# Attention with mixture of experts: row sums once a quarter, pair sums on VectorE, three jobs moved to ScalarE

## The reference

```
xn = layernorm(x)
q, k, v = xn @ W.T + b                      # 16 heads of 32
s = q.k / sqrt(32), causal, minus slope[h] * |i - j|
attn = (softmax(s) @ v) @ Wo.T + bo
logits = xn @ gate_w.T; top 2 of softmax(logits), their weights normalised
ffn = sum over both: weight * (silu(xn @ w1g.T) * (xn @ w1u.T)) @ w2.T
out = x + attn + ffn
```

## Time and profile before

| | |
|---|---|
| median of 3 runs | 1599.04 us (1596.22 to 1602.14) |
| profiled execution | 1600.13 us, span 1598.3 us |
| TensorE busy | 1465.1 us, 92% of the span |
| VectorE busy | 936.9 us, 59% |
| ScalarE busy | 703.9 us, 44% |
| GpSimd busy | 848.4 us, 53% |
| groups 0 to 14 | from 75 to 1068 us |
| last group, then its tail | 1068 to 1118 us, then to about 1175 us |

### The profile page before, as it was taken

How to read it: one execution, slowest core, us unless ns; L and a number is a source line. 1 busy time by engine, 2 the same in 40 slices (tenths; PEclk the granted TensorE clock), 3 DMA queues, 4 the chain that set the end, 5 groups by cost and what they waited for, 6 DMA issues and landing times.

```text
span 1598.3 us, 35194 instructions
## 1 busy us (share of the span) xinstructions
PE 1465.1 (92%) x13499; PEld 862.9 (54%) x13499; DVE 936.9 (59%) x1765; ACT 703.9 (44%) x1179; POOL 848.4 (53%) x732
## 2 busy tenths in 40 slices
PE   4689989998998999999999899897789999999995
PEld 2356555654655565555565456553356565655663
DVE  7667877766687666668768976560143333333331
ACT  5245565545556555556664444465022222222221
POOL 5134555444454454545564446575117777668774
PEclk9899998999998999999999999998899999999998
DMA  7244433443524426343233310233867888889983
GB/s 252 57 130 135 140 94 108 119 132 105 161 81 116 136 85 209 92 126 102 89 107 112 100 41 16 68 126 101 303 161 131 133 129 137 125 120 148 147 138 44
DMA packets 189309, 193.92 MB, mean 121 GB/s; under 512 B 104900, under 2 KB 138948, under 8 KB 189021
## 3 DMA queue, kind: packets, MB, share of 16 engines
q1 hardware_dynamic: 160636, 152.27, 35.6%
q0 software_dynamic: 26128, 37.24, 14.0%
q10 hardware_dynamic: 2384, 2.16, 0.4%
HBM read 93.14 MB, written 53.74 MB: 92 GB/s over the span
## 4 chain that ended last, share of the span: by engine, by line
PE 67%; DVE 11%; DMA 8%; ACT 4%; issue 4%; POOL 3%; SPq 2%; ACTq 0%; another core or an unknown queue 0%; DVEq 0%; POOLq 0%
PE S L1356 13%; PE T L1205 4%; PE S L1205 4%; PE M L1284 4%; PE O L1387 4%; PE M L1387 4%; PE S L1238 3%; DVE arena L1671 3%; PE T L1238 3%; PE S L1266 3%; DMA arena<-arena 3%; PE O L1284 3%; DMA out<-arena 2%; PE T L1222 2%; PE T L1318 2%
## 5 line engine op out<-in xcount | busy, mean ns | idle before, releaser
L1864 ACT ACTIVATE arena<-S,psl 128x512 f32<-128x512 f32 (+1 forms) x640 | 401.8, 642 | 359.2 <-PE S L1268 194.4
L1984 POOL TENSOR_TENSOR arena<-arena 128x1024 f32<-128x1024 f32 (+1 forms) x160 | 312.3, 1954 | 215.9 <-ACT arena L1864 215.4
L2038 POOL DMA_INDIRECT out<-arena x142 | 222.1, 1564 | 110.2 <-issue 46.7
L1356 PE MATMUL S<-arena 128*128 x1704 | 267.4, 314 | 6.1 <-issue 4.9
L1671 DVE TENSOR_REDUCE arena<-S 128x1 f32<-128x512 f32 (+3 forms) x311 | 202.8, 656 | 103.5 <-PE S L1243 53.2
L1671 DVE TENSOR_REDUCE arena<-T 128x1 f32<-128x512 f32 (+3 forms) x297 | 193.7, 656 | 87.1 <-PE T L1243 49.1
L1356 PEld LDWEIGHTS S<-arena 128*128 128x128 f16 x1704 | 166.8, 98 | 103.7 <-issue 7.4
L1266 PE MATMUL S<-arena 106*128 106x256 f16 x640 | 179.3, 280 | 22.4 <-ACT arena L1864 21.2
L1973 POOL TENSOR_TENSOR arena<-arena 128x512 f16<-128x512 f32 x64 | 78.9, 1233 | 153.9 <-DVE arena L1644 153.7
L1783 DVE COPY arena<-T 128x512 f16<-128x512 f16 x71 | 30.2, 425 | 219.8 <-PE T L1371 181.9
L1238 PE MATMUL T<-arena 105*128 105x512 f16 (+3 forms) x382 | 113.1, 333 | 25.0 <-DMA arena<-in_up 10.1
(11 more groups left out here) (218 smaller groups left out, 2517.3 us busy)
## 6 DMA issues: line engine op xcount, KB each, us to landing
arena<-arena SPq DMA_DIRECT2D x192, 128.0 KB, 2.8
arena<-in_w1T SPq DMA_DIRECT2D x64, 352.0 KB, 3.6
arena<-in_x SPq DMA_DIRECT2D x64, 256.0 KB, 4.4
w_d<-arena SPq DMA_DIRECT2D x32, 352.0 KB, 2.8
arena<-w_d SPq DMA_DIRECT2D x16, 704.0 KB, 6.7
arena<-in_w2T SPq DMA_DIRECT2D x32, 256.0 KB, 3.0
out<-arena SPq DMA_DIRECT2D x32, 256.0 KB, 3.2
xn_d<-arena SPq DMA_DIRECT2D x24, 256.0 KB, 2.6
```

The costliest lines, as they stand in the source:

```text
L1356: tp = pe.matmul(y[:, i * 512:i * 512 + I], xT[:, s % XDEEP, 4 * a + c, :], weights[:, bass.ds(reg[s] + (w_ * NX * W1N + c * 2 * I + i * I ...
L1864: act.activation(PT[t % 3][:, h, 0:n], CB[o.bank["score", u]][:, 0:n], ACT.Exp, scale=psl[:, hh:hh + 1]).then_inc(sems["exp"], 1)
L1984: pool.tensor_tensor(PS[t % 3][:, :, f:f + n], PT[t % 3][:, :, f:f + n], PT[t % 3][:, :, c:c + n], ALU.add).then_inc(sems["add"], 1)
L2038: pool.indirect_dma_start(out=halves, out_offset=bass.IndirectOffsetOnAxis(row[:, part, s:s + 1].bitcast(U32), 0), in_=yo[:, s % YDEEP, c0 ...
```

## The change

- `rsum` is made once a quarter instead of once a quad: of AC, the sum over all key blocks of the quarter. It is placed right behind the first product with V of the next quarter; for the very last quad it stays where it was.
- GpSimd still adds the key halves of each quad: for the first of a quarter straight into AC (two buffers), for the others into PSF (off the diagonal) or PSD (diagonal). On the diagonal it has two instructions of 128x512 where it had one.
- New step `acc` on VectorE for all quads but the first of a quarter, placed at u + 4: AC += PSF (128x1024), or the right half of AC += PSD (128x512).
- `vsb` and `qkh` move from VectorE to ScalarE. V is copied without its bias. New step `aTh` on ScalarE adds the bias (`bvs`) to the quotient, twice (128x256 each): rounded into aT and in place; GpSimd's `aT` keeps only the subtraction.
- `aTh` comes a unit behind `a32`, `aT` another; `inverse` comes 4 units behind `osb` instead of 3. `wsl` comes a unit later, its store doesn't.
- The broadcast of the V bias at the start and its buffer go; buffers shift by 512 words, which moves one expert weight load from window 3 to window 4.

```
@@ score, products, sums @@
             at(u + 1, lambda: add("add", t))
+            if i:
+                at(u + 4, lambda: add("acc", t))
             at(4 * t + 5, lambda: products(t))
-            at(4 * t + (10 if i < q else 9), lambda: sums(t))
+            if t == QUADS - 1:
+                at(4 * t + 9, lambda: sums(t))
...
         add("pv", t)
+        if i == 0 and t:
+            sums(t - 1)
...
         add("rsum", t)
-        if i == q:
-            at(now[0] + 1, lambda: emptied(G, q))
+        at(now[0] + 1, lambda: emptied(G, q))
@@ emptied @@
-                add("aT", G, q)
-                ready["aT", G, q] = now[0] + 2
+                at(now[0] + 1, lambda: add("aTh", G, q))
+                at(now[0] + 2, lambda: add("aT", G, q))
+                ready["aT", G, q] = now[0] + 4
...
-        at(now[0] + 3, inverse)
+        at(now[0] + 4, inverse)
@@ w_split @@
             yield
+            yield
             add("wsl", i)
-            for _ in range(2):
-                yield
+            yield
             add("wstore", i, sem="wd", inc=16)
@@ sync @@
-                    sp.dma_start(bvb[:, :], T["bv"].partition_broadcast(P)).then_inc(sems["bb"], 16)
@@ tensor, rsum @@
+                if i:
+                    on.wait_ge(*at("acc", t))
                 for x in range(4):
-                    R = YB[o.bank["pv", G, q]][D * x:D * x + D, 2 * P:4 * P]
-                    if i < q:
-                        tp = pe.matmul(R, ones, PS[t % 3][:, x, :], start=False, stop=False)
-                    else:
-                        pe.matmul(R[:, 0:P], ones, PT[t % 3][:, x, 0:P], start=False, stop=False)
-                        tp = pe.matmul(R[:, P:2 * P], ones, PS[t % 3][:, x, P:2 * P], start=False, stop=True)
+                    tp = pe.matmul(YB[o.bank["pv", G, q]][D * x:D * x + D, 2 * P:4 * P], ones, AC[q % 2][:, x, :],
+                                   start=False, stop=True)
@@ vector @@
+            elif kind == "acc":
+                t, = key
+                G, q, i = quad(t)
+                on.wait_ge(*at("add", t))
+                f, z = (0, PSF) if i < q else (P, PSD)
+                if i > 1:
+                    on.wait_ge(*at("acc", t - 1))
+                dve.tensor_tensor(AC[q % 2][:, :, f:], AC[q % 2][:, :, f:], z, ALU.add).then_inc(sems["acc"], 1)
@@ scalar @@
+                act.activation(st[:, 2 * qk, lo:hi], t32_at(*key), ACT.Copy).then_inc(sems["qkh"], 1)
...
+                act.activation(V[(G + 1) % 3][:, 4 * half:4 * half + 4, :].rearrange("p a n -> p (a n)"),
+                               PB[o.bank["v", b, g, half]][:, :], ACT.Copy, scale=col(CV)).then_inc(sems["vsb"], 1)
...
+                on.wait_ge(*at("a32", G, q))
...
+                a_ = osb[:, q % 2, 0:2 * P]
+                act.activation(aT[:, 0, g, 2 * q * P:2 * (q + 1) * P], a_, ACT.Identity, bias=bvs[:, g:g + 1])
+                act.activation(a_, a_, ACT.Identity, bias=bvs[:, g:g + 1]).then_inc(sems["aTh"], 1)
@@ gpsimd, add @@
+                if i == 0:
...
+                    f, n = (0, 2 * P) if q else (P, P)
+                    if q == 0:
+                        pool.tensor_copy(z[:, :, 0:P], y[:, :, 0:P])
+                    pool.tensor_tensor(z[:, :, f:f + n], y[:, :, f:f + n], y[:, :, 2 * P:2 * P + n],
+                                       ALU.add).then_inc(sems["add"], 1)
+                elif i < q:
+                    if t > 10:
+                        on.wait_ge(*at("acc", t - 1 if i == 2 else t - 3 if q == 3 else t - 6))
+                    elif i == 2 or q == 3:
+                        on.wait_ge(*at("acc", t - 1 if i == 2 else t - 3))
+                    pool.tensor_tensor(PSF, y[:, :, 0:2 * P], y[:, :, 2 * P:4 * P], ALU.add).then_inc(sems["add"], 1)
+                else:
+                    if G or q > 1:
+                        on.wait_ge(*at("acc", t - (3, 3, 4)[q - 1]))
+                    pool.tensor_tensor(PSD, y[:, :, P:2 * P], y[:, :, 2 * P:3 * P], ALU.add)
...
+                    pool.tensor_tensor(z[:, :, 0:P], z[:, :, 0:P], y[:, :, 0:P], ALU.add).then_inc(sems["add"], 1)
@@ gpsimd, aT @@
-                then(pool.tensor_copy(d0, osb[:, q % 2, 0:2 * P]))
                 pool.tensor_tensor(d1, osb[:, q % 2, 0:2 * P], d0, ALU.subtract).then_inc(sems["aT"], 1)
```

More of the change, by code:

```diff
@@ L878, in build @@
     xh, to = place(to, [P, 3, 2 * E], F16)
-    bvb, to = place(to, [P, E], F32)
     EARLY = to
@@ L886, in build @@
     PT1, to = place(to, [P, 4, 512], F32)
-    PS0, to = place(to, [P, 4, 2 * P], F32)
+    AC0, to = place(to, [P, 4, 2 * P], F32)
     RAWO_AT = to
-    PS1, to = place(to, [P, 4, 2 * P], F32)
+    AC1, to = place(to, [P, 4, 2 * P], F32)
     V2, to = place(to, [P, 8, P], F32)
@@ L893, in build @@
     AFTER_PT = to
-    PS2, to = place(to, [P, 4, 2 * P], F32)
+    PSF, to = place(to, [P, 4, 2 * P], F32)
+    PSD, to = place(to, [P, 4, P], F32)
     V1, to = place(to, [P, 8, P], F32)
@@ L1635, in vector @@
                                   PB[o.bank["gate", b]][:, 0:64], col(IG), None, ALU.mult).then_inc(sems["lg"], 1)
-            elif kind == "qkh":
-                b, g, qk, half = key
-                lo, hi = half * 512, half * 512 + 512
-                on.wait_ge(*at("qk32", *key))
-                if b * NG + g:
-                    gb, gg = (b, g - 1) if g else (b - 1, NG - 1)
-                    for h in range(4):
-                        on.wait_ge(*at("stack", gb, gg, h))
-                dve.tensor_copy(st[:, 2 * qk, lo:hi], t32_at(*key)).then_inc(sems["qkh"], 1)
-            elif kind == "vsb":
-                b, g, half = key
-                on.wait_ge(*at("v", b, g, half, 3))
-                on.wait_ge(sems["bb"], 32)
-                G = b * NG + g
-                if G > 2:
-                    on.wait_ge(*at("pv", 10 * (G - 2) - 1))
-                elif G == 2:
-                    on.wait_ge(*at("place", 1))
-                    on.wait_ge(*at("place", 2))
-                elif G == 1:
-                    on.wait_ge(*at("wol", 1))
-                dve.scalar_tensor_tensor(
-                    V[(G + 1) % 3][:, 4 * half:4 * half + 4, :],
-                    PB[o.bank["v", b, g, half]][:, :].rearrange("p (a n) -> p a n", a=4), col(CV),
-                    bvb[:, g * P:(g + 1) * P].unsqueeze(1).to_broadcast([P, 4, P]), ALU.mult,
-                    ALU.add).then_inc(sems["vsb"], 1)
             elif kind == "mx":
@@ L1843, in scalar @@
                                scale=cs).then_inc(sems["qk32"], 1)
+            elif kind == "qkh":
+                b, g, qk, half = key
+                lo, hi = half * 512, half * 512 + 512
+                on.wait_ge(*at("qk32", *key))
+                if b * NG + g:
+                    gb, gg = (b, g - 1) if g else (b - 1, NG - 1)
+                    for h in range(4):
+                        on.wait_ge(*at("stack", gb, gg, h))
+                act.activation(st[:, 2 * qk, lo:hi], t32_at(*key), ACT.Copy).then_inc(sems["qkh"], 1)
+            elif kind == "vsb":
+                b, g, half = key
+                on.wait_ge(*at("v", b, g, half, 3))
+                on.wait_ge(*at("scales", 1))
+                G = b * NG + g
+                if G > 2:
+                    on.wait_ge(*at("pv", 10 * (G - 2) - 1))
+                elif G == 2:
+                    on.wait_ge(*at("place", 1))
+                    on.wait_ge(*at("place", 2))
+                elif G == 1:
+                    on.wait_ge(*at("wol", 1))
+                act.activation(V[(G + 1) % 3][:, 4 * half:4 * half + 4, :].rearrange("p a n -> p (a n)"),
+                               PB[o.bank["v", b, g, half]][:, :], ACT.Copy, scale=col(CV)).then_inc(sems["vsb"], 1)
+            elif kind == "aTh":
+                G, q = key
+                b, g = G // NG, G % NG
+                on.wait_ge(*at("a32", G, q))
+                if b:
+                    on.wait_ge(*at("o", b - 1, 2 * q, 2))
+                    on.wait_ge(*at("o", b - 1, 2 * q + 1, 2))
+                a_ = osb[:, q % 2, 0:2 * P]
+                act.activation(aT[:, 0, g, 2 * q * P:2 * (q + 1) * P], a_, ACT.Identity, bias=bvs[:, g:g + 1])
+                act.activation(a_, a_, ACT.Identity, bias=bvs[:, g:g + 1]).then_inc(sems["aTh"], 1)
             elif kind == "exp":
@@ L1851, in scalar @@
                     on.wait_ge(*at("add", t - 3))
-                    if quad(t - 3)[1] == quad(t - 3)[2]:
-                        on.wait_ge(*at("rsum", t - 3))
                 elif t == 2:
```

28 lines of the change are left out of this document (14 added, 14 removed).

## The result

The changed kernel took 1609.07 us (median of 4 runs, 1606.28 to 1610.55), the kernel before beside it 1597.88 us (4 runs); the ratio is 1.0088, 95% interval 1.0054 to 1.0123. So it is slower by 0.9%, where the prediction had 1554 us, 2.8% faster. The profiled span is 1608.3 us against 1598.3.

A forecast was written before the change was run, and what follows sets the result against it. TensorE, busy 95% of the attention stage, was taken as the bound. 59.4 + 3 + 1 + 2 - 9 - 8 - 2 - 1 = 45.4 us off 1600.13 gave 1554.7, set at 1554 us; range 1536 to 1580.

The forecast's parts named there:

- 59.4 us: Attention, TensorE: fewer row-sum sets save 59.4 us over the 15 groups that TensorE bounds.
- the rival that TensorE's gain isn't the time's: Attention: exponential, GpSimd sum and maxima set the pace together, so gaps just grow; 1592 to 1600 us, chance 6%.
- -8 us: Attention, VectorE: net +51 us of work makes TensorE wait longer for the maxima, 8 us lost.
- The rival in which the lock makes VectorE the bound: Attention: every `acc` waits out a whole GpSimd sum on the shared SBUF port; 1625 us, chance 4%.
- hidden: Attention, GpSimd: net +49 us of work costs no time, since its sums wait for exponentials anyway.
- -9 us: Attention, ScalarE: 160 inserted instructions, one in ten delaying an exponential without slack, lose 9 us.
- the second rival: ScalarE's `aTh`, in the exponentials' queue, waits for the normalised rows instead of GpSimd; 1577 us, chance 20%.
- +3: Attention, TensorE: row-sum sets of off-diagonal quads stop waiting for GpSimd's sums, 3 us gained.
- +1: One queue entry less at the start and roundings off VectorE while it is saturated, 1 us gained.
- +2: Last group: the reciprocal placed later means less waiting for the fold ahead of the exponentials, 2 us gained.
- -2: Routing's split low part comes a unit later, its store doesn't, leaving less time to land: 2 us lost.
- All of it arrives: Attention: slack swallows VectorE's and ScalarE's added loads, and the last group gains too; 1533 us, chance 15%.

The follow-up runs named there:

- run 9: Kernel before with row-sum sets only for diagonal quads, 64 instead of 160, multiplying a constant; 1565.70 us, 0.982.
- run 10: run 9 plus, in `acc`'s place, a one-input VectorE sum along the row that waits for its GpSimd sum; 1601.21 us, 1.003.
- run 4: Changed kernel with the 48 large `acc` cut from 128x1024 to 128x4, order and semaphores kept; 1578.99 us, 0.9917.
- run 2: Kernel before with only the moves: `qkh`, `vsb` and the two additions of `aTh` on ScalarE; 1593.27 us, 0.9994.
- run 12: run 9 plus the three moves to ScalarE; 1562.64 us, 0.9792.
- run 1: Changed kernel without the moves: `qkh` and `vsb` back on VectorE, `aT` back on GpSimd alone; 1614.28 us, 1.0121.
- run 7: run 6 without the moves, the V copy as in run 1; 1641.82 us, 1.028.
- run 6: Changed kernel without `acc`: GpSimd adds both halves of every quad to the running sum, moves kept; 1627.16 us, 1.0207.
- run 11: run 9 plus GpSimd's extra sums, the diagonal pair sums of 48 later quads made twice; 1572.66 us, 0.9869.
- run 3: Changed kernel with `aTh` directly behind `a32` and `aT` one unit earlier; 1617.51 us, 1.0136.
- run 8: Changed kernel with the spreading product `bc` and what follows (`a32`, `aTh`, `aT`) two units earlier; 1619.33 us, 1.0144.
- run 5: Changed kernel with the 48 large `acc` as one-input sums along the row of the same 128x1024; 1604.15 us, 1.0061.
- run 14: Changed kernel with every `acc` one unit earlier in VectorE's queue; 1643.54 us, 1.0288.

## Why the prediction was wrong, point by point

**The row sums, "59.4 us".** This is the first step that failed. The count of the sets and their cost were right to a sixth (50.7 of 59.4 us): TensorE's busy time fell by 50.7 us in run 9. But the step took TensorE's time for the kernel's. Run 9 gives 30.6 us (1596.32 to 1565.70), with VectorE, ScalarE and GpSimd doing the work that they did before. The prediction read 53 us of gaps in 993 as "TensorE is the bound"; it set a chance of 6% on the rival that TensorE's gain isn't the time's. About half of that rival is what happens: the gaps grow by a third of the saving (16.9 of 50.7 us) even before any engine gets more to do. A small sum of waits tells how often the others are late now, not how soon they would be.

**VectorE, "-8 us".** This step failed by more, and it turned the sign. The durations were good: `acc` was put at 1.59 and 0.80 us and took 1.415 and 0.905, 111.4 us in all against 114.7. The price was not: run 10 sets it at 35.5 us for 63 us more busy time in the stage (70 in the span), and run 4 gives 27 us back for 54. That is some 0.5 us of time for 1 us of VectorE, waits included, at an engine busy 72 to 78% of the stage. Of the 40 us by which run 10's stage is longer, 15.7 are TensorE's own busy time at the lower mean clock, the rest its gaps. The prediction had -8 for a net load of 51 us, 0.16 for 1, by letting the 23.2 us of waits grow by a third; they grew to 55.1 us. It also set the rounding and V copies that leave VectorE against `acc` one for one. The runs say that they are worth much less: in runs 2 and 12 VectorE loses 69 to 71 us (and GpSimd some 23) and the time 0 to 3 us, with ScalarE's load of some 90 us as the other side. Where VectorE or GpSimd has more to do, the same moves give more: 5 us from run 1 to the change, not clear of noise, and 12 us from run 7 to run 6, which is. Whether a gain on VectorE and a loss on ScalarE cancel was not tried by itself; the waits point to it (TensorE's waits from run 9 to run 12, for VectorE 35.0 to 28.5 us, for ScalarE 25.4 to 40.2 us; from run 1 to the change, 72.9 to 55.1 and 22.0 to 42.7).

**The lock.** Its row was read rightly, but for one figure: L1725 was through 0.76 us after the sum (462.12 against 461.36), not 0.95. The rival in which the lock makes VectorE the bound did not come: `acc` would have had to average 3 us, and its mean is 1.16. Undisturbed (the medians, 1.21 and 0.68 us) the 96 would be 90.7 us, so by this estimate the lock adds 20.7 us to them. It strikes others as well, the 128x1 at 347.44 and the layer norm's L1553 at 239.97; both stand ahead of maxima. In sum that is nothing new for L1553: its 32 have a mean of 850 ns here and 924 in the kernel before. The Trainium skill says in SBUF — State Buffer, section "SBUF: two separate sides", that the one who comes second on the shared port pair stands still for the other's whole instruction; both rows agree: L1704 took 2.21 us for one element per partition beside a sum with 2.20 us to go, and L1553, which takes 0.54 us undisturbed (its median), was through 0.29 us after its sum.

**GpSimd, "hidden".** The load was 69 us in the whole span (49 predicted), and run 11 prices 58 us of it, in the stage, at 7.0 us. Runs 6 and 7 show the same with more. In the time this is a small miss, but the reason given, that GpSimd waits for exponentials anyway, doesn't hold where its instructions hold up VectorE.

**ScalarE, "-9 us", and the second rival.** The additions took 0.50 us, not 0.40, and ScalarE's busy time grew by 96 us in the span, not 113. TensorE waits 32.7 us for the exponentials, close to the 35 that the prediction had set as the mark of that rival. Its waits for ScalarE come with the moves: in run 1, without them, TensorE waits 22.0 us for ScalarE, in the change 42.7. So the forecast of more waits was right, and more came than the 9 us. Yet runs 2 and 12 show that the moves by themselves cost no time, and without them TensorE waits about as much longer for VectorE. So more waits for ScalarE are not by themselves more time. A part, such as the wait of `osb` at 243.08, needs late GpSimd steps and ScalarE's new place together; what it costs is not shown, since run 3 left that wait as it was and run 8 put others in its place.

**The small terms and one rival's sum.** +3, +1, +2, -2 and -1 were not tried one by one. The waits for GpSimd's sums behind +3 are gone (2.5 us of the matmuls' waits in the stage before, none after). Outside the stage the forecast was of the right size: ahead of the first score the change is 1.3 us shorter (75.4 to 74.1 us), behind group 14 it is 1.8 us shorter (530.0 to 528.2). -2 can't be read from any run. The rival "All of it arrives" adds the 4 us of the last group in words and 2 in its sum; with 4 it is 1531, not 1533. Neither bears on the result.

**What the prediction said would show it.** "Groups unchanged at 66 us with more gaps on TensorE, or layer norm groups longer than before by more than 3 us" was named as the sign of a wrong forecast; a mix of both came: 67.1 us a group, three layer norm groups longer by 3.2 to 6.6 us.

**What stays open.** The difference between the parts' sum and the whole (6 us with the moves, 7 without, at the edge of the intervals). One candidate is the lock on `acc`, which run 10 leaves out; in run 5 the large ones without it are 0.3% faster, not clear of noise. And how much of the 35 us is plain time in the queue and how much is waiting behind late sums. Run 10 has only 13.9 us of waits of the new instructions and none of GpSimd for them, and costs 35.5 us; run 14 has the change's instructions, with 20 us more of `acc`'s waits in the stage (40.3) and 24 us less of GpSimd's (8.4), and costs 32 us more. So both count, and no run keeps one and takes away the other. No complete kernel tried beats the kernel before; the one that matches it is run 2.

## What to carry to other kernels

Before counting a saving on the busiest engine as time, ask what each microsecond costs on the engine that would be next: here 31 of TensorE's 51 us arrived, 0.6 for 1, and each microsecond put on VectorE, busy 75% of the stage (run 9), cost some 0.5. At these rates, which are those of this kernel, the large accumulation takes 1.41 us for 0.66 us of TensorE, an estimated 0.7 us of time for 0.4, and so loses without any misplaced step. In a fixed order across engines, put new work where nothing urgent stands behind its wait, and try one unit to either side: the same `acc` one unit earlier cost 2% more.

## What the runs showed of the hardware

The granted clock takes back a part of what gaps leave. After the gap of 6.08 us at 344.4 to 350.5, TensorE runs at the lower of its levels; in the kernel before it has no gap from 339 to 358 us, and the clock there is 1.00. Busy time by window, then timeline, of the changed kernel:

```profile
339.00:344.00 5.00, 4.37 (x36) 1.84 (x34) 2.90 (x10) 1.85 (x3) 0.44 (x1) 1.00 0.23 64
350.00:353.00 3.00, 2.48 (x7) 0.83 (x8) 2.35 (x4) 1.19 (x2) 0.00 (x0) 0.50 0.00 1
353.00:358.00 5.00, 5.00 (x41) 2.92 (x40) 4.47 (x7) 2.38 (x5) 3.34 (x2) 0.85 0.35 108
```

```profile
343.13 1.03 PE L1321 MATMUL S<-arena 128*128 128x512 f16 x4
...
351.51 1.91 PE L1321 MATMUL S<-arena 128*128 128x512 f16 x4
```

At 0.50 (1.2 GHz of 2.4) four products of 128x512 take 1.91 us instead of 1.03. So this gap of 6 us costs some 2 us more behind it, by an estimate from the rows: half of 2.48 us and 0.15 of 5.00 us. In sums: runs 9 and 10 have the same instructions on TensorE, and it is busy 888.8 us at 0.97 in the one and 904.5 at 0.95 in the other, 15.7 us more for the same work.

The lock doesn't look at size: 128x1 with two SBUF inputs (L1704) lasted 2.21 us beside a GpSimd sum, and its neighbour of the same shape and kind (L1705), right behind the end of that sum, 0.16 us. An instruction with one input of 128x1024 was never held up: 48 in run 5 and 48 in run 10 all took 1.20 to 1.22 us.
